# Audio tower on one core: the order of Gram products, tile 1's remainders and the first norm before the loop

## The chip, the cores and the metric

The kernel runs on one core of a Trainium2 chip. The metric is the device time of one execution in microseconds (us), and the median of several executions is what is compared. The engines are named as the profile names them: PE (matrix multiplication), PEld (its weight loads), DVE (vector), ACT (scalar), POOL (GpSimd), and SP, which issues most transfers. Each works through its own list of instructions in order, and they wait for one another on semaphores.

## The reference, cut to what matters

A path of 64 sequences by 64 steps with 8 channels is turned into signatures up to level 4, projected to 128 features, and followed by an attention block and a mixture of experts:

```python
h = _L0_tok_ref(x, L0_tok_W, L0_tok_b)          # signatures: levels 1..4, then sigs @ W.T + b
h = h + _L0_attn_ref(_layernorm(h), w_qkv, u_qkv, sigma_qkv, w_out, b_out, u_out, sigma_out, temperature)
h = h + _L0_ffn_ref(_layernorm(h), gate_w, w1, w2, w3, sw1, sw2)   # top-1 of 8 experts + a shared one

# one signature step, v = increment of the path
e = [v]; e.append(_outer(e[-1], v) / (k + 1))    # k = 1..3
acc = levels[k] + e[k] + sum(_outer(levels[i], e[k - 1 - i]))

# spectral norm of w_qkv and of w_out, one step of power iteration
v = W @ u; v = v / norm(v); u2 = W.T @ v; u2 = u2 / norm(u2)
W_used = W / (v @ W @ u2) * sigma
```

The 4,096 tokens are 32 tiles of 128. All is fp32.

## The kernel before, in words

The running sums over time are matrix products with a triangular matrix (`before`, `upto`). Level 1 and level 2 are made for many tiles at once: level 2 in four groups of eight tiles (`sum_level2(n)` on PE, `add_s2(n)` on DVE). Level 3 and the level 4 input are made tile by tile: POOL or DVE writes the outer product `e3`, ACT its high part `e3h`, POOL or DVE the remainder `e3l`, PE sums both (`sum_level3`), DVE adds `g4` (`level4`, writes `u4`), PE transposes (`features`), ACT copies the high part (`uth`, `lowt`) and DVE writes the remainders (`features_lo`, writes `utl` and `lowt`). `project(s, lo, hi)` multiplies tile s by the signature weights: ten steps n, of which 0 to 4 fill bank 1 and 5 to 9 bank 2; a step with n different from 4 and 9 is three multiplications, and steps 4 and 9 (`wlow`) are two. DVE weighs the two banks by the channels (`weigh`, writes `z`), POOL adds the eight channels in three additions (`add_channels`, the tree), and PE sums over time (`accumulate`). Then comes the first norm: DVE `first_norm`, POOL a root, DVE `first_norm_finish`, which writes `xn`; PE transposes it (`x_columns`).

A loop over 32 tiles overlaps all of this: iteration i does the attention of tile i, projects tile i+2 and starts tile i+3. Before the loop stands a hand-written prologue that fills this pipeline. It also makes the products of attention weights, and the two spectral norms from Gram matrices: `gram_qkv` is twelve products of 128x128 fp32, each two passes in the trace, all summed in bank 5, and `gram_wout` does the same for `w_out`. `norm_mm` counts the norm's matrix products as done, and `norm_step` DVE's steps of the norm.

The order on each engine is that of the code. The change touches the prologue on PE (around L1459 to L1487) and on DVE (L1076 to L1092). Three waits of the prologue matter below. `project(1, 0, ...)` waits for both remainders of tile 1 (`u4_lo`). `x_columns(0)` waits for `xn_ready`, and everything behind it on PE, `sum_level3(2)` and the second half of tile 1's projection, stands behind that wait. POOL's `level3_rest(2)` computes `g4` directly behind the root, then waits for `xn_ready` before it writes `e3l`.

Of the kernel before, what the change touches and what calls it, by code (L numbers as in the profile page):

```python
# [39 lines left out]
P = 128  # L40
# [5 lines left out]
INNER = HEADS * HEAD_DIM  # L46
# [10 lines left out]
UC = C3 // P  # L57
# [6 lines left out]
SECOND_GROUP_STEPS = 17  # L64
# [14 lines left out]
def spread(ap, axis, shape):  # L79

    return ap.unsqueeze(axis).to_broadcast(shape)
# [7 lines left out]
def build(nc, x_next, x_prev, w_low, w_high, tok_b, wqkv, u_qkv, wout_t, u_columns, b_out,  # L89
          scalars, gate_t, w13_t, w2_t, sw1_t, sw2_t, square, mask_c, steps, out):  # L90
    with ExitStack() as ctx:
# [3 lines left out]
        def sem(name):  # L95
            return ctx.enter_context(nc.semaphore(name))
# [111 lines left out]
        def taker(*hosts):  # L208
# [3 lines left out]
            def take(*shape):  # L212
# [3 lines left out]
                for part in parts:  # L216
                    flat, at = part
                    if at + size <= flat.shape[1]:
# [3 lines left out]
                        if len(shape) == 1:  # L222
# [64 lines left out]
        norm_root, norm_mm, norm_step, exp_temp = (sem("norm_root"), sem("norm_matmul"), sem("norm_step"),  # L287
                                                   sem("exp_temperature"))
# [474 lines left out]
        def _(d):  # L763
# [3 lines left out]
            def step(ins):  # L767

                nonlocal n_small
                ins.then_inc(small, 1)  # L770
                n_small += 1
                return n_small

            def after(n):
                d.wait_ge(small, n)

            def remainder(out_, x_, hi, done):

                return V.tensor_tensor(out_, x_, hi.bitcast(F32), ALU.subtract).then_inc(done, 1)  # L779

            def outer(out_, left, right):
                shape = [P, left.shape[1], CHANNELS, CHANNELS]
                return V.tensor_tensor(out_.rearrange("p t (a c) -> p t a c", c=CHANNELS), spread(left, 3, shape),
                                       spread(right, 2, shape), ALU.mult)
# [11 lines left out]
            def low_outer(ts):  # L796
                return step(outer(low[:, ts, 1 + CHANNELS:LOW], t3[:, ts, :], vh[:, ts, :]))
# [5 lines left out]
            def add_s2(n, then=None):  # L803

                s2 = B[SUM_BANKS[n]][:].rearrange("p (t c) -> p t c", c=C2)
                d.wait_ge(s2_psum, n + 1)
                made = step(V.tensor_tensor(low[:, groups[n], 1 + CHANNELS:LOW],
                                            low[:, groups[n], 1 + CHANNELS:LOW], s2, ALU.add))
                if then:
                    then(made)  # L810
                if n:
                    d.wait_ge(g3_outer, 1)
                return step(V.tensor_tensor(g3[:, groups[n], :], g3[:, groups[n], :], s2, ALU.add))
# [28 lines left out]
            made = step(V.tensor_scalar(v3, v[:], 1.0 / 3.0, None, ALU.mult))  # L842
# [3 lines left out]
            made = add_s2(0, first_level3)  # L846
# [32 lines left out]
            def weigh(s, half, first=False):  # L879

                cs = slice(half * 4, half * 4 + 4)
                d.wait_ge(y_psum, 2 * s + (half + 1))
                if half == 0 and not first:
                    d.wait_ge(tree, 3 * s - 2)
                V.tensor_tensor(z[:, cs, :], B[1 + half][:].rearrange("p (c d) -> p c d", c=4),  # L885
                                spread(v[:, bass.ds(s, 1), cs].rearrange("p o c -> p (o c)"), 2, [P, 4, DIM]),
                                ALU.mult).then_inc(z_sb, 1)

            def tile_h(t):
                return one(h[:, bass.ds(t, 1), :])  # L890

            def first_norm(t):
                d.wait_ge(h_psum, t + 1)
                V.tensor_tensor(h1[:], B[3][:, P:P + DIM], tokb[:], ALU.add).then_inc(h_read, 1)  # L894
                d.wait_ge(h_read, t + 1)
                V.bn_stats(stats[:, 0, :], h1[:]).then_inc(ln1, 1)

                d.wait_ge(ln1, 3 * t + 1)
                V.tensor_tensor(tile_h(t), B[3][:, P:P + DIM], tokbout[:], ALU.add).then_inc(h_biased, 1)
                V.bn_aggr(meanvar[:, 0, :], stats[:, 0, :]).then_inc(ln1, 1)  # L900
                d.wait_ge(ln1, 3 * t + 2)
                V.tensor_scalar(rstd[:, 0, 0:1], meanvar[:, 0, 1:2], EPS, None, ALU.add).then_inc(ln1, 1)

            def first_norm_finish(t):
                d.wait_ge(rooted[0], t + 1)
                V.tensor_scalar(xn[:], h1[:], meanvar[:, 0, 0:1], rstd[:, 0, 1:2], ALU.subtract, ALU.mult) \  # L906
                    .then_inc(xn_ready, 1)
# [5 lines left out]
            def features_lo(s):  # L913
                d.wait_ge(u4_hi, 2 * s + 2)
                remainder(utl[:].rearrange("p c t -> p (c t)"), B[0][:], uth[:].rearrange("p c t -> p (c t)"),
                          u4_lo)
                rows_ = slice(C2, P)
                remainder(lowt[rows_, 0, :], B[3][rows_, 0:P], lowt[rows_, 0, :], u4_lo)
                rows_ = slice(C2 + 2 * FEW_STEP, STACKED)
                remainder(lowt[rows_, 1, :], B[3][rows_, 3 * P:], lowt[rows_, 1, :], u4_lo)  # L920
# [136 lines left out]
            made = nstep(V.tensor_tensor(gram_u, B[5][:, 0:DIM], uq[:], ALU.mult))  # L1057
# [17 lines left out]
            d.wait_ge(consts_cast, 3)  # L1075
            weigh(0, 0, True)  # L1076
            weigh(0, 1)
            rest_made = low_outer(slice(per, TILES))
            features_lo(1)
            first_norm(0)  # L1080
            first_norm_finish(0)
            after(rest_made)
            made = add_s2(1)
            assert made == SECOND_GROUP_STEPS

            d.wait_ge(norm_mm, 2)
            V.tensor_copy(gram_out, B[5][:, 0:DIM])
            made = nstep(V.tensor_copy(wu_out[:], B[5][:, DIM:DIM + 1]))
            assert made == OUT_COLUMN_STEP
            V.tensor_tensor(nrm[:, 0:1], ucol[:, 0:1], wtwu[:], ALU.mult)  # L1090
            V.tensor_tensor(nrm[:, 1:2], wtwu[:], wtwu[:], ALU.mult)
            V.tensor_tensor(nrm[:, 2:3], wu_out[:], wu_out[:], ALU.mult)  # L1092
# [2 lines left out]
            made = nstep(V.tensor_tensor(nrm[:, 3:4], wu_out[:], B[5][:, DIM + 1:DIM + 2], ALU.mult))  # L1095
            assert made == SUMS_STEP
            made = add_s2(3)
# [7 lines left out]
            made = nstep(V.tensor_tensor(fac[:, 2:4], B[6][:, 256:260][:, 0:4:2], fac[:, 6:8], ALU.mult))  # L1105
# [110 lines left out]
        def _(pe):  # L1216
# [23 lines left out]
            def weight_products(banks, left, right):  # L1240

                for c in range(PAIRS):
                    for n in range(2):
                        rows_ = slice(n * HEAD_DIM, (n + 1) * HEAD_DIM)
                        last = mm(banks[n][:, col(c)], wqkv_sb[rows_, left + c, :], right[rows_, c, :])
                        if c == PAIRS - 1:
                            last.then_inc(ww_psum, 1)

            def gram_qkv():

                nq = 3 * INNER // P
                for c in range(nq):
                    last = mm(B[5][:, 0:DIM], wqkv_sb[:, c, :], wqkv_sb[:, c, :], c == 0, c == nq - 1)
                last.then_inc(norm_mm, 1)

            def gram_wout():

# [7 lines left out]
            def sum_level3(s):  # L1265


                pe.wait_ge(e3_lo, s + 1)
                mm(B[0][:], before_r[:], e3h[:], True, False)
                mm(B[0][:], before_r[:], e3l[:], False, True).then_inc(s3_psum, 1)  # L1270
# [12 lines left out]
            def project(s, lo, hi):  # L1283

                if lo == 0:
                    pe.wait_ge(z_sb, 2 * s)
                    pe.wait_ge(u4_hi, 2 * s + 2)
                    pe.wait_ge(u4_lo, 3 * s + 3)
                for n in range(lo, hi):
                    half_, c = divmod(n, UC + 1)  # L1290
                    bank, cols = B[1 + half_][:], col(half_, 512)
                    if c < UC:
                        mm(bank, uth[:, c, :], whigh[:, 0, c, cols], c == 0, False)
                        mm(bank, uth[:, c, :], whigh[:, 1, c, cols], False, False)
                        mm(bank, utl[:, c, :], whigh[:, 0, c, cols], False, False)
                    else:
                        mm(bank, lowt[:, 0, :], wlow[:, 0, cols], False, False)
                        mm(bank, lowt[0:STACKED, 1, :], wlow[0:STACKED, 1, cols], False, True).then_inc(y_psum, 1)
# [160 lines left out]
            sum_level2(0)  # L1459
            pe.wait_ge(ld_w, 16)  # L1460
            weight_products(B[6:8], PAIRS, wqkv_sb[:, 0:PAIRS, :])
            pe.wait_ge(before_cast, 1)
            sum_level3(0)
            pe.wait_ge(ld_sq, 32)
            features(0, False)
            gram_qkv()
            project_first_hi(0)
            sum_level3(1)
            pe.wait_ge(ld_wo, 16)
# [9 lines left out]
            pe.wait_ge(ww_lo, 2)  # L1479
            sum_level2(3)  # L1480
            gram_wout()
            project(1, 0, 1)
            accumulate(0)
            project(1, 1, UC + 1)
            pe.wait_ge(norm_step, OUT_COLUMN_STEP)
            mm(B[5][:, DIM + 1:DIM + 2], gram_out, wu_out[:]).then_inc(norm_mm, 1)
            x_columns(0)  # L1487
# [169 lines left out]
```

## Time and profile before

| | |
|---|---|
| median of 3 executions | 667.78 us (665.4 to 669.15) |
| profiled execution, its own time | 667.03 us |
| its span | 665.2 us |
| PE busy | 639.6 us, 96% of the span |
| DVE, POOL, ACT busy | 62%, 48%, 43% |
| share of PE in the chain that ended last | 91% |
| prologue, start to the first matmul of iteration 0 | 45.01 us |

Rows of the timeline give the start in us from the span's start, the length in us, the engine and line, the operation with its tiles, and in brackets the engine's idle time just before and what ended it. A length of PE counts to the modelled end of the last matmul of the row, so the difference of two starts is the better measure of work. The profile shows fp32 matmuls of 128x128 as two passes each. `PEclk` is the TensorE clock that was granted, where 1.00 stands for 2.4 GHz and 0.50 for 1.2 GHz.

### The profile page before, as it was taken

The numbers are of one execution on the slowest core, as the hardware profiler recorded it, in microseconds if no ns is written. First come the engines' busy times: TensorE is split into PE (matmuls) and PEld (weight loads), VectorE is DVE, ScalarE is ACT, GpSimd is POOL, SyncE is SP. The second block draws the span as 40 slices with busy tenths as digits, with TensorE's granted clock in tenths as the row PEclk, the third lists the DMA queues.
The fourth block names the chain that finished last, engine by engine and source line by source line (L and its number), as shares of the span: only waits on it lengthen the run. The fifth ranks groups of instructions, "written<-read, shape, count | busy, mean of one in ns | idle before, by whom it ended". The sixth has DMA issues, their size and how long they took to land.

```text
span 665.2 us, 14412 instructions
## 1 busy us (share of the span) xinstructions
PE 639.6 (96%) x4269; PEld 535.5 (81%) x4270; DVE 411.6 (62%) x1064; ACT 286.1 (43%) x655; POOL 320.6 (48%) x336
## 2 busy tenths in 40 slices
PE   5999999999999999999999999999998999999993
PEld 3777888878888878888878888877678999999993
DVE  7966666666666666666666667687646224455550
ACT  4334444454444454444444444453473433344431
POOL 2455444545444545444545444545747105555553
PEclk9989999999999999999999999999999999999997
DMA  8611433443633443433443433111337322333330
GB/s 304 237 69 30 109 80 79 113 93 83 139 79 79 114 92 83 107 79 80 114 92 83 107 79 80 41 35 45 100 97 243 94 64 38 47 46 45 44 47 2
DMA packets 70133, 59.70 MB, mean 90 GB/s; under 512 B 6752, under 2 KB 58848, under 8 KB 69728
## 3 DMA queue, kind: packets, MB, share of 16 engines
q1 hardware_dynamic: 63472, 55.21, 32.5%
q0 software_dynamic: 6640, 4.22, 4.7%
q8 instruction: 12, 0.20, 0.1%
q14 instruction: 9, 0.07, 0.0%
HBM read 16.78 MB, written 26.30 MB: 65 GB/s over the span
## 4 chain that ended last, share of the span: by engine, by line
PE 91%; DVE 4%; POOL 2%; issue 1%; ACT 0%; DMA 0%; DVEq 0%; SPq 0%; POOLq 0%
PE bank L1220 83%; PE bank L1276 2%; PE bank L1433 2%; PE bank L1403 1%; POOL z L472 1%; PE bank L1531 1%; PE bank L1326 1%; PE bank L1335 1%; PE bank L1281 1%; PE bank L1280 1%; POOL z L474 0%; DVE z L885 0%; DVE ident_b L1068 0%; DMA h<-x_prev 0%; DVE whigh L779 0%
## 5 line engine op out<-in xcount | busy, mean ns | idle before, releaser
L1220 PE MATMUL bank<-whigh,uth 128*128 128x512 f32 x512 | 169.1, 411 | 1.2 <-DVE lowt L779 1.2
L1220 PEld LDWEIGHTS bank<-whigh,uth 128*128 128x128 f32 x512 | 92.2, 190 | 28.0 <-issue 7.4
L1220 PE MATMUL bank<-whigh,utl 128*128 128x512 f32 x256 | 101.7, 397 | 0.0
L559 POOL DMA_INDIRECT out<-prob,ids x39 | 60.7, 1557 | 78.2 <-ACT prob L740 76.5
L481 POOL TENSOR_TENSOR rstd<-rstd,powers 128x1 f32<-128x1 f32 x64 | 35.2, 550 | 123.5 <-DVE rstd L872 67.3
L472 POOL TENSOR_TENSOR z<-z 128x512 f32<-128x512 f32 x32 | 42.1, 1316 | 89.6 <-DVE z L885 89.6
L1220 PE MATMUL bank<-xvo,x 128*128 128x128 f32 x624 | 76.3, 275 | 0.5 <-DVE x L1175 0.3
L1220 PEld LDWEIGHTS bank<-xvo,x 128*128 128x128 f32 x624 | 72.8, 192 | 0.9 <-DVE x L1175 0.4
L1220 PE MATMUL bank<-xT,qkw 128*128 128x128 f32 x512 | 62.5, 275 | 1.0 <-ACT pt L645 1.0
L1220 PEld LDWEIGHTS bank<-xT,qkw 128*128 128x128 f32 x512 | 59.7, 192 | 1.5 <-issue 1.4
L1191 DVE TENSOR_TENSOR z<-tail,bank 128x512 f32<-128x512 f32 x39 | 26.8, 688 | 50.6 <-PE bank L1220 50.6
L1220 PEld LDWEIGHTS bank<-whigh,utl 128*128 128x128 f32 x256 | 48.5, 189 | 12.0
L885 DVE TENSOR_TENSOR z<-bank,v 128x512 f32<-128x512 f32 x64 | 44.2, 691 | 20.4 <-PE bank L1220 16.6
L633 ACT ACTIVATE prob<-prob 128x512 f32<-128x512 f32 x32 | 20.2, 633 | 63.6 <-DVE prob L1011 63.6
L611 ACT ACTIVATE xqk<-bank,fac 128x512 f32<-128x512 f32 x64 | 44.0, 689 | 7.8 <-PE bank L1220 6.5
L645 ACT COPY pt<-bank 128x512 f32<-128x512 f32 x32 | 18.8, 586 | 65.8 <-PE bank L1433 65.8
L1220 PEld LDWEIGHTS bank<-xvp,pt 128*64 128x64 f32 x512 | 30.1, 137 | 18.1 <-issue 18.1
L467 POOL TENSOR_TENSOR e3l<-e,e3h 128x512 fp32r<-128x512 f32 x31 | 40.4, 1304 | 6.7 <-DVE xn L906 5.4
L894 DVE TENSOR_TENSOR h<-bank,tokb 128x128 f32<-128x128 f32 x32 | 9.3, 292 | 54.4 <-PE bank L1220 54.3
L1220 PE MATMUL bank<-vow,xTh 128*128 128x512 f32 x128 | 42.9, 416 | 0.0
L620 ACT COPY xvo<-bank 128x512 f32<-128x512 f32 x64 | 37.6, 588 | 10.6 <-PE bank L1220 8.9
L1220 PE MATMUL bank<-levels,z 128*128 x312 | 41.5, 276 | 0.0
(223 smaller groups left out, 1319.3 us busy)
## 6 DMA issues: line engine op xcount, KB each, us to landing
sorted_rows<-blank SPq DMA_DIRECT2D x24, 709.5 KB, 5.9
xvp<-xvo SPq DMA_DIRECT2D x128, 128.0 KB, 2.3
w<-w_t SPq DMA_DIRECT2D x1, 4096.0 KB, 12.1
xvo<-sorted_rows SPq DMA_DIRECT2D x39, 64.5 KB, 1.8
w<-w_high SPq DMA_DIRECT2D x4, 512.0 KB, 6.3
x_columns<-x2t SPq DMA_DIRECT2D x32, 64.0 KB, 1.6
xg_in<-x_columns SPq DMA_DIRECT2D x8, 256.0 KB, 4.9
levels<-w_t SPq DMA_DIRECT2D x1, 2048.0 KB, 8.9
```

What stands on the lines that cost most here:

```text
L467: G.tensor_tensor(e3l[:], e3[:], e3h[:].bitcast(F32), ALU.subtract).then_inc(e3_lo, 1)
L472: G.tensor_tensor(z4[:], z[:, 0:4, :], z[:, 4:8, :], ALU.add).then_inc(tree, 1)
L481: G.tensor_tensor(rstd[:, n, 1:2], rstd[:, n, 0:1], powers[:, 0:1], ALU.pow) \
L559: nc.gpsimd.indirect_dma_start(out=out[:, :], out_offset=bass.IndirectOffsetOnAxis(ap=ids[:, j:j + 1], axis=0), in_=y[:, 2 if j == SORTED ...
L611: A.activation(xqk[:, :, 4 * n:4 * n + 4, :], B[5 + n][:].rearrange("p (s h k) -> p s h k", s=2, h=4), ACT.Copy, scale=fac[:, 1:2]).then_i ...
L620: A.copy(xvo[:, n, :, :].rearrange("p c d -> p (c d)"), B[7 - 2 * n][:]) \
L633: A.activation(prob[:], prob[:], ACT.Exp).then_inc(exp_done, 1)
L645: A.copy(pt[:].rearrange("k c s q -> k (c s q)"), B[6][:]).then_inc(pT_sb, 1)
L885: V.tensor_tensor(z[:, cs, :], B[1 + half][:].rearrange("p (c d) -> p c d", c=4), spread(v[:, bass.ds(s, 1), cs].rearrange("p o c -> p (o ...
L1191: V.tensor_tensor(hidT[:, k, :, :].rearrange("p c t -> p (c t)"), act[:, k, :], B[2 + 2 * k][:], ALU.mult).then_inc(hid_done, 1)
L1220: return T.matmul(out_, lhsT, rhs, start=start, stop=stop)
L1276: T.transpose(B[0][:, col(c)], u4[:, col(c)], ident)
```

## The change

It moves instructions of the prologue, and adds or removes none. On PE the twelve Gram products of `wqkv` are cut in three pieces (3, 2 and 7), two of which go ahead of and behind the first level 3 sum, and `accumulate(0)` goes from behind the first step of tile 1's projection to behind the third. On DVE tile 1's remainders go ahead of the outer product of the other 24 tiles, the copies of the second Gram product go ahead of the second group's level 2 sums, and the first norm goes behind those.

```diff
+            features_lo(1)
             rest_made = low_outer(slice(per, TILES))
-            features_lo(1)
-            first_norm(0)
-            first_norm_finish(0)
-            after(rest_made)
-            made = add_s2(1)
-            assert made == SECOND_GROUP_STEPS
-
             d.wait_ge(norm_mm, 2)
             V.tensor_copy(gram_out, B[5][:, 0:DIM])
             made = nstep(V.tensor_copy(wu_out[:], B[5][:, DIM:DIM + 1]))
             assert made == OUT_COLUMN_STEP
+            after(rest_made)
+            made = add_s2(1)
+            assert made == SECOND_GROUP_STEPS
+            first_norm(0)
+            first_norm_finish(0)
...
-            def gram_qkv():
+            def gram_qkv(lo, hi):
...
-                for c in range(nq):
+                for c in range(lo, hi):
...
             weight_products(B[6:8], PAIRS, wqkv_sb[:, 0:PAIRS, :])
+            gram_qkv(0, 3)
             pe.wait_ge(before_cast, 1)
             sum_level3(0)
+            gram_qkv(3, 5)
             pe.wait_ge(ld_sq, 32)
             features(0, False)
-            gram_qkv()
+            gram_qkv(5, 3 * INNER // P)
...
-            project(1, 0, 1)
+            project(1, 0, 3)
             accumulate(0)
-            project(1, 1, UC + 1)
+            project(1, 3, UC + 1)
```

On PE, at the first level 3 sum, the list before reads as follows (`w` is the buffer of `wqkv`; the first row is the weight products, `low_tile` the last transposes of tile 0):

```order
L1220 MATMUL bank<-w 128x128 x8
L1220 MATMUL bank<-e3h,before_r 128x512
L1220 MATMUL bank<-e3l,before_r 128x512
L1276 MATMUL bank<-sq,u 128x128 x4
L1280 MATMUL bank<-sq,low_tile 128x128
L1281 MATMUL bank<-sq,low_tile 128x128
L1220 MATMUL bank<-w 128x128 x12
```

And in the changed kernel:

```order
L1219 MATMUL bank<-w 128x128 x11
L1219 MATMUL bank<-e3h,before_r 128x512
L1219 MATMUL bank<-e3l,before_r 128x512
L1219 MATMUL bank<-w 128x128 x2
L1276 MATMUL bank<-sq,u 128x128 x4
L1280 MATMUL bank<-sq,low_tile 128x128
L1281 MATMUL bank<-sq,low_tile 128x128
L1219 MATMUL bank<-w 128x128 x7
```

Three Gram products have gone ahead of the sum and two ahead of the transposes, and seven are left behind them. Lines of the changed kernel are one lower here.

On PE, at tile 1's first half, before (`z,sq` is `accumulate(0)`, `xn` is `x_columns(0)`):

```order
L1220 MATMUL bank<-whigh,uth 128x512 x2
L1220 MATMUL bank<-whigh,utl 128x512
L1220 MATMUL bank<-z,sq 128x128
L1220 MATMUL bank<-whigh,uth 128x512 x2
L1220 MATMUL bank<-whigh,utl 128x512
L1220 MATMUL bank<-whigh,uth 128x512 x2
L1220 MATMUL bank<-whigh,utl 128x512
L1220 MATMUL bank<-whigh,uth 128x512 x2
L1220 MATMUL bank<-whigh,utl 128x512
L1220 MATMUL bank<-wlow,lowt 128x512 x2
L1220 MATMUL bank<-wu_out,x2t 128x1
L1326 MATMUL bank<-sq,xn 128x128
```

And in the changed kernel:

```order
L1219 MATMUL bank<-whigh,uth 128x512 x2
L1219 MATMUL bank<-whigh,utl 128x512
L1219 MATMUL bank<-whigh,uth 128x512 x2
L1219 MATMUL bank<-whigh,utl 128x512
L1219 MATMUL bank<-whigh,uth 128x512 x2
L1219 MATMUL bank<-whigh,utl 128x512
L1219 MATMUL bank<-z,sq 128x128
L1219 MATMUL bank<-whigh,uth 128x512 x2
L1219 MATMUL bank<-whigh,utl 128x512
L1219 MATMUL bank<-wlow,lowt 128x512 x2
L1219 MATMUL bank<-wu_out,x2t 128x1
L1326 MATMUL bank<-sq,xn 128x128
```

`accumulate(0)` has moved behind six more multiplications; five instead of eleven are left between it and the product with `wu_out`.

On DVE, behind tile 0's weighing (the first common row), before and after in one piece (L783 is the outer product of 24 tiles, L779 the remainders, L807 and L813 are `add_s2(1)`):

```order
 L885 TENSOR_TENSOR z<-bank,v 128x512 x2
+L779 TENSOR_TENSOR utl<-bank,uth 128x512
+L779 TENSOR_TENSOR lowt<-bank,lowt 64x128
+L779 TENSOR_TENSOR lowt<-bank,lowt 9x128
 L783 TENSOR_TENSOR levels<-x,vh 128x24x64
-L779 TENSOR_TENSOR utl<-bank,uth 128x512
-L779 TENSOR_TENSOR lowt<-bank,lowt 64x128
-L779 TENSOR_TENSOR lowt<-bank,lowt 9x128
-L894 TENSOR_TENSOR h<-bank,tokb 128x128
-L896 BN_STATS stats<-h 128x6
-L899 TENSOR_TENSOR h<-bank,tokbout 128x128
-L900 BN_AGGR meanvar<-stats 128x2
```

The remainders come first now, and the norm (L894 on) no longer follows them; it stands behind the outer product, two copies and `add_s2(1)`.

## Rows read from the trace of the kernel before

**Rows 1.** The page: busy time of each engine.

```profile
PE 639.6 (96%) x4269; PEld 535.5 (81%) x4270; DVE 411.6 (62%) x1064; ACT 286.1 (43%) x655; POOL 320.6 (48%) x336
```

**Rows 2.** Windows inside the loop: stretch and its length, busy times, PEclk, DMA.

```profile
100.00:300.00 200.00, 200.00 (x1250) 160.35 (x1250) 131.97 (x365) 89.74 (x210) 97.60 (x112) 1.00 0.41 95
```

**Rows 3.** Timeline of PE from the weight products to tile 0's projection.

```profile
11.54 0.76 PE L1220 MATMUL bank<-e3h,before_r 128*128 128x512 f32 x1 [1.15 <-DVE e3l L849]
...
13.61 1.08 PE L1276 MATMUL bank<-sq,u 128*128 128x128 f32 x4 [0.88 <-DVE u L829]
...
14.91 4.47 PE L1220 MATMUL bank<-w 128*128 128x128 f32 x24
19.14 0.48 PE L1220 MATMUL bank<-whigh,uth 128*128 128x512 f32 x1
```

**Rows 4.** Timeline of DVE around the first Gram matrix.

```profile
17.68 0.62 DVE L779 TENSOR_TENSOR lowt<-bank,lowt 64x128 fp32r<-64x128 f32 x2
19.49 0.29 DVE L1057 TENSOR_TENSOR x2n<-bank,uq 128x128 f32<-128x128 f32 x1 [1.19 <-PE bank L1220]
```

**Rows 5.** Timeline of PE from tile 1's projection to iteration 0.

```profile
33.82 0.71 PE L1220 MATMUL bank<-whigh,uth 128*128 128x512 f32 x2 [1.24 <-DVE lowt L779]
...
34.95 0.49 PE L1220 MATMUL bank<-z,sq 128*128 128x128 f32 x2 [0.19 <-POOL z L476]
...
40.31 0.48 PE L1220 MATMUL bank<-e3h,before_r 128*128 128x512 f32 x1
...
41.56 0.62 PE L1220 MATMUL bank<-whigh,uth 128*128 128x512 f32 x2
...
42.26 0.63 PE L1220 MATMUL bank<-whigh,uth 128*128 128x512 f32 x2
...
45.01 1.95 PE L1220 MATMUL bank<-xT,qkw 128*128 128x128 f32 x16
```

**Rows 6.** Windows of one us around the fall of the clock, columns as in rows 2.

```profile
35.00:36.00 1.00, 1.00 (x4) 0.85 (x5) 0.49 (x2) 0.04 (x1) 0.93 (x1) 0.69 0.76 328
36.00:37.00 1.00, 1.00 (x4) 0.76 (x3) 0.63 (x4) 0.95 (x3) 0.22 (x1) 0.50 0.01 0
...
38.00:39.00 1.00, 1.00 (x4) 0.77 (x4) 1.00 (x2) 0.00 (x0) 0.77 (x2) 0.61 0.03 8
```

**Rows 7.** Timeline of ACT: high part of tile 1.

```profile
30.57 0.38 ACT L590 CAST lowt<-bank 128x256 fp32r<-128x256 f32 x1
```

**Rows 8.** Timeline of DVE from the outer product to the norm's columns.

```profile
30.68 1.74 DVE L783 TENSOR_TENSOR levels<-x,vh 128x1536 f32<-128x1536 f32 x1
32.35 0.68 DVE L779 TENSOR_TENSOR utl<-bank,uth 128x512 fp32r<-128x512 f32 x1
...
35.48 0.29 DVE L894 TENSOR_TENSOR h<-bank,tokb 128x128 f32<-128x128 f32 x1 [1.80 <-PE bank L1220]
...
37.38 1.10 DVE L906 TENSOR_SCALAR xn<-h,meanvar,rstd 128x128 f32<-128x128 f32 x1 [0.68 <-POOL rstd L481]
38.41 0.68 DVE L807 TENSOR_TENSOR levels<-levels,bank 128x512 f32<-128x512 f32 x1
...
39.60 0.28 DVE L1087 COPY x2t<-bank 128x128 f32<-128x128 f32 x1
...
39.98 0.16 DVE L1090 TENSOR_TENSOR nrm<-ucol,wtwu 128x1 f32<-128x1 f32 x1
```

**Rows 9.** Timeline of POOL: the tree, the root, g4 and e3l.

```profile
30.84 2.71 POOL L472 TENSOR_TENSOR z<-z 128x512 f32<-128x512 f32 x1 [3.09 <-DVE z L885]
...
34.44 0.46 POOL L476 TENSOR_TENSOR z<-z 128x128 f32<-128x128 f32 x1
...
36.78 0.57 POOL L481 TENSOR_TENSOR rstd<-rstd,powers 128x1 f32<-128x1 f32 x1 [0.85 <-DVE rstd L902]
37.34 1.07 POOL L461 TENSOR_TENSOR g<-levels,vh 128x512 f32<-128x512 f32 x1
38.63 1.28 POOL L467 TENSOR_TENSOR e3l<-e,e3h 128x512 fp32r<-128x512 f32 x1 [0.23 <-DVE xn L906]
```

More of the change, by code:

```diff
@@ L1247, in weight_products @@
                             last.then_inc(ww_psum, 1)
-            def gram_qkv():
+            def gram_qkv(lo, hi):
                 nq = 3 * INNER // P
-                for c in range(nq):
+                for c in range(lo, hi):
                     last = mm(B[5][:, 0:DIM], wqkv_sb[:, c, :], wqkv_sb[:, c, :], c == 0, c == nq - 1)
-                last.then_inc(norm_mm, 1)
+                if hi == nq:
+                    last.then_inc(norm_mm, 1)
             def gram_wout():
```

## The prediction

> **What bounds the kernel now.** I read the page first. PE is busy 96% of the span [rows 1], and in the loop it is busy without a gap at the full clock: 200.00 of 200 us [rows 2]. So whatever starts the loop earlier or later by some amount moves the end by that amount, and nothing in this change touches the loop itself. What is to be found is when iteration 0 begins; now it is 45.01 us [rows 5]. I then read the timelines of the prologue, engine by engine, for PE's gaps. There are gaps of 1.15 and 0.88 us around the first level 3 sum [rows 3], one of 1.24 before tile 1's projection and one of 0.19 before `accumulate(0)` [rows 5]. Last I read the windows: the clock goes from 1.00 to 0.69 and 0.50 about one and a half microseconds after the 1.24 gap has ended, stays at 1.2 GHz, and is back in the stretch that begins at 38 [rows 6]. By the shares of those windows it fell at 35.4 and rose at 38.8: some 3.4 us at half speed, which cost about 1.7 us of work.
>
> **Gram products.** PE did the twelve in 19.14 - 14.91 = 4.23 us, 0.176 per pass [rows 3]. Three products are six passes, 1.06 us, and fit the gap of 1.15. Two are 0.70 and fit the gap of 0.88. If those passes are slower because the clock is still low there, up to 0.22 each (as the six transposes from 13.61 to 14.91 took [rows 3]), they overrun the first gap by 0.15 us and the second not at all; the remainder e3l is what the sum waits for anyway. So tile 0's transposes stay at 13.61, and the seven left end at about 14.91 + 14 x 0.176 = 17.4 (up to 18.0). PE can't use all of this. Next comes tile 0's projection, which waits for DVE's last remainder; that ends at 17.68 + 0.62 = 18.30 [rows 4]. PE begins at 18.45 in place of 19.14: **-0.7 us on PE**, and a new gap of 0.5 to 1 us, more if the clock rises early, stands before it. DVE's wait of 1.19 us for the first Gram matrix [rows 4] goes, so DVE is 1.2 us earlier from there. That is also what the outer product on POOL and the weight remainders follow. PE has no gap from 19.14 to 32.58, the start of the 1.24 gap, so its 0.7 arrives there whole: PE is free for tile 1 at 31.9.
>
> **Tile 1's remainders.** DVE ends the weighing of tile 0 at about 30.77 now, as POOL's tree starts at 30.84 [rows 9]; 1.2 earlier is 29.6, and PE's banks allow it. ACT has the high parts of tile 1 at 30.57 + 0.38 = 30.95 [rows 7], with PE's 0.7 at 30.25. Then the remainders run at 30.3, without the outer product's 32.35 - 30.68 = 1.67 us ahead of them [rows 8]. From their start to PE's start it takes 33.82 - 32.35 = 1.47 [rows 5, 8], so 31.8; PE itself is free at 31.9. **Tile 1's projection starts at 31.9 in place of 33.82, -1.9 us, and the 1.24 gap is gone**, and with it the reason for the fall of the clock at 35.3.
>
> **accumulate(0).** Nine multiplications are ahead of it instead of three. A step of three takes 42.26 - 41.56 = 0.70 at the full clock [rows 5], so PE is there at 34.0. Is the tree ready? Now it starts at 30.84 and its first addition takes 2.71 [rows 9], ending 1.2 behind the end of the outer product at 32.35. I read this as POOL having waited for DVE's outer product. In the change the outer product starts at 31.6 at the earliest and falls among the tree's three additions. Whether they wait for each other or not, from the start at 29.7 the tree can't take longer than its 4.1 us now (30.84 to 34.90 [rows 9]) plus some tenths: 33.9 at the latest, 32.3 without a wait. Both are before 34.0. So `accumulate(0)` is at 34.05 in place of 34.95: -0.9.
>
> **The norm behind it decides.** DVE could take the sum at 34.6 (0.53 behind `accumulate(0)`, as 35.48 behind 34.95 [rows 5, 8]). But it now stands behind the outer product (31.6, pushed to about 31.75 by POOL, + 1.67 = 33.4), the two copies (39.98 - 39.60 = 0.38) and `add_s2(1)` (39.60 - 38.41 = 1.19) [rows 8]: 35.0. So the norm starts at 35.0 in place of 35.48, -0.45. From here on the chain is the same: statistics, root at +1.30 (36.78), POOL's g4 directly behind it, `xn`, then e3l, which ends at 38.63 + 1.28 = 39.91, 4.43 behind the norm's start [rows 8, 9]. That gives 39.5 for `sum_level3(2)` in place of 40.31: **-0.8**.
>
> For the `xn` step I take 1.10 [rows 8]. It lies over g4, from 37.34 to 38.41 [rows 9], and DVE's next instruction starts at 38.41. The order of both engines is unchanged here, so g4 will be ahead of it again. The Trainium skill ("SBUF — State Buffer", Who interferes with whom) says that DVE in a two-port mode and GpSimd exclude each other for a whole instruction, whoever is first. By that rule the 1.10 stays, and the trace agrees with it in this row; if the two could overlap, `xn` would come up to 0.8 us earlier and the norm's wait on PE would shrink by as much, though e3l would still stand behind g4.
>
> **What PE does meanwhile.** Behind `accumulate(0)` only five multiplications (1.2 us) and the small product with `wu_out` are left, whose column DVE has written at 33.8. PE is out of work at about 35.8 and waits in `x_columns(0)` for `xn` until 38.0, then in `sum_level3(2)` until 39.5. That is some 3.5 us of gaps with a transpose between them, where before there were 1.24 + 0.19 and 0.46 us. The twelve multiplications of tile 1's second half stand behind these waits. The stall has moved, not gone.
>
> From `sum_level3(2)` to iteration 0 it is 45.01 - 40.31 = 4.70 us at the full clock [rows 5]. After a gap of 1.24 the clock was at half speed for 3.4 us; after 3.5 us of gaps I expect it to fall as well, at some point around 38 to 39, and to stay down for about as long. The part that falls on work, 2.5 to 3.4 us at half speed, costs 1.3 to 1.7; I take 1.5. Iteration 0 then starts at 39.5 + 4.7 + 1.5 = 45.7 in place of 45.01. **The sum is +0.7 us** (-0.8 for the chain, +1.5 for the clock).
>
> The Trainium skill ("TensorE: Matmul & The Clock Gate", What's actually happening) has the same rule: idle time halves the clock, and only sustained activity restores it. It speaks against this change, since it turns two short gaps into one long one.
>
> **Its size.** The profiled execution took 667.03 by its own time, so 667.7; against the median of 667.78 it is 668.5. The two anchors differ by as much as the sum, so I put down 668.2. A difference of 0.5%, 3.3 us, is about what a measurement of this kernel can tell from no change; the three runs of before spread over 3.7 us.
>
> **Rivals.**
> 1. *The gain arrives whole (chance 0.15).* The clock doesn't fall, or not while PE has work, as PE has been busy without a gap from 18.45 to 35.8. Then only the chain counts: -0.8, 666.2 to 667.0. If in addition `xn` came earlier (the norm's 4.43 us has 1.07 of g4 in it), it would be up to -1.9, 665.1 to 665.9. For it speaks that the 1.24 gap vanishes; against it the chain through the norm, in which no row gets shorter.
> 2. *The clock stays low through all of tile 1's second half (0.25), the slower side.* It decides if the clock doesn't return until `features(2)`. Fourteen multiplications of 512 columns and the transposes, the 4.7 us, then cost up to 4.7 more: -0.8 + 4.7 = +3.9 at the worst, 670.9 to 671.7; with return half way +2, 669.0 to 669.8. For it speaks that PE is idle for most of 35.8 to 39.5; against it that the low stretch of before ended while PE worked on.
> 3. *The change does nothing that shows (0.1).* The new gap before 18.45 makes the clock fall there as well, by the same 1.7 us that the old gap cost later, or the DVE's outer product is pushed behind the tree, so that the norm starts at 35.5. Then all moves cancel: 667.0 to 668.0.
> 4. *The forecast (0.5):* the norm starts 0.45 earlier, the clock falls behind the new wait and comes back: +0.2 to +1.5, 667.2 to 669.3.
>
> **How the numbers follow.** None of the four cases is sure to leave the band of 3.3 us; only the worst end of rival 2 (+3.9) does, and the scatter of runs adds to it. Faster by over 0.5% has 0.05, the tail of rival 1 with the scatter. Slower by over 0.5% has 0.09. The rest is 0.86 for within 0.5%. The range leaves out the ends of rivals 1 and 2: 665.9 to 670.6.
>
> **What would show it.** Right: tile 1's projection starts near 31.9 without a gap; DVE goes from L779 (`lowt`, 18.3) to L1057 at once; `x_columns(0)` has a gap of about 2 us released by `xn`, and PEclk is at 0.5 somewhere between 38 and 43; iteration 0 starts between 45 and 46.5. Wrong: a start of `first_norm` before 34.7 (then DVE wasn't the limit), no fall of the clock (rival 1), or half clock up to iteration 0 (rival 2). A change in the loop's own period would be outside all of this.

## The result and the profile after

The change is slower by 0.3%: ratio of the changed kernel to the kernel before 1.0032, 95% interval [1.0019, 1.0046], medians 668.70 us and 667.62 us over ten executions each. Those medians are 1.1 us apart and the means 1.7, where the ratio stands for 2.1 us, so the size is less sure than the sign. Run again in a later series it gave 1.0036 [1.0021, 1.0050]. The forecast was 668.2 us, 0.5 below the median, and the range of 665.9 to 670.6 held it.

The profiled execution of the changed kernel has a span of 665.5 us. Its timeline of PE, with the rows that answer to [rows 3] and [rows 5]:

```profile
11.49 0.47 PE L1219 MATMUL bank<-e3h,before_r 128*128 128x512 f32 x1 [0.54 <-DVE e3l L849]
...
13.30 0.63 PE L1276 MATMUL bank<-sq,u 128*128 128x128 f32 x4 [0.65 <-DVE u L829]
...
13.98 1.73 PE L1219 MATMUL bank<-w 128*128 128x128 f32 x14
17.99 0.47 PE L1219 MATMUL bank<-whigh,uth 128*128 128x512 f32 x1 [2.29 <-issue]
...
31.34 0.70 PE L1219 MATMUL bank<-whigh,uth 128*128 128x512 f32 x2
...
33.52 0.38 PE L1219 MATMUL bank<-z,sq 128*128 128x128 f32 x2
...
37.66 0.47 PE L1326 MATMUL bank<-sq,xn 128*128 128x128 f32 x1 [2.47 <-DVE xn L906]
39.07 0.80 PE L1219 MATMUL bank<-e3h,before_r 128*128 128x512 f32 x1 [0.94 <-POOL e3l L467]
...
45.92 1.95 PE L1219 MATMUL bank<-xT,qkw 128*128 128x128 f32 x16
```

The seven Gram products left (14 passes) end early, and PE then has a gap of 2.29 us before tile 0's projection, for which the profile names no releaser; DVE's last remainder of tile 0 ends at 17.9. The 1.24 gap before tile 1's projection is gone: it starts at 31.34 in place of 33.82, and `accumulate(0)` at 33.52 in place of 34.95. Then come the two new waits, 2.47 us for `xn` and 0.94 for `e3l`. Of the lead of 2.48 us at 31.34, 1.24 is left at `sum_level3(2)` (39.07 against 40.31), and at iteration 0 PE is 0.91 us late (45.92 against 45.01). The windows say what became of it, with the columns of rows 2:

```profile
36.00:37.00 1.00, 0.00 (x0) 0.00 (x0) 0.49 (x1) 0.00 (x0) 1.00 (x2) 0.99 0.00 0
37.00:38.00 1.00, 0.34 (x1) 0.18 (x1) 1.00 (x5) 0.00 (x0) 0.77 (x2) 0.50 0.00 0
42.00:43.00 1.00, 1.00 (x4) 0.80 (x3) 0.00 (x0) 0.00 (x0) 0.00 (x0) 0.50 0.00 0
43.00:44.00 1.00, 1.00 (x4) 0.77 (x3) 0.00 (x0) 0.00 (x0) 0.00 (x0) 0.59 0.00 0
```

The clock fell to 1.2 GHz at 37.0, in the middle of the wait for `xn`, and rose again at 43.8. `sum_level3(2)` to iteration 0 took 6.85 us in place of 4.70, 2.15 more. The span is only 0.3 us longer than before (665.5 against 665.2), though iteration 0 is 0.91 us late: the loop's 31 steps to the last iteration take the same 438.3 us, and what stands behind them took 0.7 us less here. So one profile shows the prologue well and the total badly.

DVE and POOL answer to [rows 4], [rows 8] and [rows 9]:

```profile
17.92 0.29 DVE L1057 TENSOR_TENSOR x2n<-bank,uq 128x128 f32<-128x128 f32 x1
...
29.85 0.69 DVE L779 TENSOR_TENSOR utl<-bank,uth 128x512 fp32r<-128x512 f32 x1 [0.65 <-ACT lowt L590]
...
31.23 1.76 DVE L783 TENSOR_TENSOR levels<-x,vh 128x1536 f32<-128x1536 f32 x1
...
34.61 0.28 DVE L894 TENSOR_TENSOR h<-bank,tokb 128x128 f32<-128x128 f32 x1
...
36.51 1.09 DVE L906 TENSOR_SCALAR xn<-h,meanvar,rstd 128x128 f32<-128x128 f32 x1 [0.68 <-POOL rstd L481]
```

```profile
29.28 1.27 POOL L472 TENSOR_TENSOR z<-z 128x512 f32<-128x512 f32 x1 [3.09 <-DVE z L885]
...
31.43 1.88 POOL L476 TENSOR_TENSOR z<-z 128x128 f32<-128x128 f32 x1
...
37.74 1.27 POOL L467 TENSOR_TENSOR e3l<-e,e3h 128x512 fp32r<-128x512 f32 x1 [0.23 <-DVE xn L906]
```

L1057 follows without a wait, and the norm (L894) starts without one too: DVE comes to it only at 34.61, though `accumulate(0)` was at 33.52. The tree's first addition takes 1.27 us now in place of 2.71, and its third 1.88 in place of 0.46, since it lies over the outer product, which starts at 31.23. So the collision has moved from the first addition to the third.

### The profile page after: what moved, and what is told of

Same layout as the page of the kernel before. It is cut to its first block, busy times and chain, and to the rows that moved or that the text cites. A ratio compares the mean times of both kernels' runs of the same rounds, so it can differ in the third digit from the quotient of the medians.

```text
span 665.5 us, 14380 instructions
## 1 busy us (share of the span) xinstructions
PE 632.4 (95%) x4237; PEld 533.9 (80%) x4270; DVE 411.5 (62%) x1064; ACT 286.1 (43%) x655; POOL 320.9 (48%) x336
## 4 chain that ended last, share of the span: by engine, by line
PE 91%; DVE 3%; issue 2%; POOL 1%; ACT 1%; DMA 0%; SPq 0%; POOLq 0%; DVEq 0%
PE bank L1219 84%; PE bank L1276 2%; PE bank L1433 2%; PE bank L1533 1%; PE bank L1335 1%; PE bank L1326 1%; PE bank L1281 1%; PE bank L1280 1%; DVE levels L783 0%; POOL z L472 0%; DMA h<-x_prev 0%; POOL z L474 0%; POOL out L559 0%; DVE z L885 0%; DVE levels L807 0%
## 5 line engine op out<-in xcount | busy, mean ns | idle before, releaser
L894 DVE TENSOR_TENSOR h<-bank,tokb 128x128 f32<-128x128 f32 x32 | 9.3, 291 | 52.6 <-PE bank L1219 52.5
```

## The experiments

Theory A: PE's waits for `xn` and `e3l` stand in front of tile 1's second half, nothing shortens the chain that ends them, and the clock falls behind them. The rivals were that the Gram cut itself costs (C), that something behind the wait is as late (B), and that the half clock costs nothing. The ratio given is to the kernel before, run beside it on the same chip.

**The Gram cut alone.** The kernel before with this:

```diff
             weight_products(B[6:8], PAIRS, wqkv_sb[:, 0:PAIRS, :])
+            gram_qkv(0, 3)
             sum_level3(0)
+            gram_qkv(3, 5)
             features(0, False)
-            gram_qkv()
+            gram_qkv(5, 3 * INNER // P)
```

> The kernel before with only the cut of the Gram products (3, 2 and 7). Theory A (the cost lies in PE's wait for xn and e3l in front of tile 1's second half, and in the half clock behind it): this part is a gain by itself. DVE loses its wait of 1.19 us for the first Gram matrix, tile 1's projection starts 0.7 to 1.2 us earlier than 33.82, iteration 0 at 43.8 to 44.3 in place of 45.01, ratio to before 0.998 to 0.999. Rival C (the new gap of about 2.3 us before tile 0's projection costs, by the clock or by what it delays): iteration 0 not earlier than 45.0, ratio 1.000 or above.

Measured: 0.9980 [0.9971, 0.9989]. In the timeline of PE iteration 0 starts at 43.63, 1.38 us earlier than before, though the same gap of 2.3 us stands before tile 0's projection:

```profile
17.99 0.47 PE L1220 MATMUL bank<-whigh,uth 128*128 128x512 f32 x1 [2.30 <-issue]
...
32.26 0.71 PE L1220 MATMUL bank<-whigh,uth 128*128 128x512 f32 x2 [0.83 <-DVE lowt L779]
...
38.62 0.38 PE L1220 MATMUL bank<-wu_out,x2t 128*128 128x1 f32 x2 [0.62 <-DVE wu_out L1088]
...
38.93 0.48 PE L1220 MATMUL bank<-e3h,before_r 128*128 128x512 f32 x1
...
43.63 1.95 PE L1220 MATMUL bank<-xT,qkw 128*128 128x128 f32 x16
```

This part is a gain. Its `sum_level3(2)` comes at 38.93, earlier than the whole change's 39.07, so the lead that the changed kernel has at that point is all the Gram cut's. DVE says why:

```profile
34.11 0.29 DVE L894 TENSOR_TENSOR h<-bank,tokb 128x128 f32<-128x128 f32 x1 [2.00 <-PE bank L1220]
```

The norm starts at 34.11 here, and at 34.61 where the other moves are added: they bring `accumulate(0)` no gain that the norm could use (33.38 here, 33.52 there) and put `add_s2(1)` ahead of the norm.

**The rest without the Gram cut.** The changed kernel with `gram_qkv()` in one piece again.

> The changed kernel with the Gram products back in one piece of twelve. Theory A: everything is about 1 us later than in the changed kernel and the wait for xn stays, so iteration 0 at 46.5 to 47.2, ratio to before 1.003 to 1.006. Rival C: without the gap before tile 0's projection it is better than the changed kernel, iteration 0 before 45.9, ratio to before 1.002 or below.

Measured: 1.0042 [1.0029, 1.0055]. Timeline of PE:

```profile
39.60 0.47 PE L1325 MATMUL bank<-sq,xn 128*128 128x128 f32 x1 [2.52 <-DVE xn L906]
41.02 0.80 PE L1219 MATMUL bank<-e3h,before_r 128*128 128x512 f32 x1 [0.94 <-POOL e3l L467]
...
48.18 1.95 PE L1219 MATMUL bank<-xT,qkw 128*128 128x128 f32 x16
```

The loss is all in the rest. The ratio is the expected one, and in the profile iteration 0 is later than expected (48.18, where at most 47.2 was): `sum_level3(2)` at 41.02 is even behind the 40.31 of before, and from there it is 7.16 us to iteration 0. Of the delay 0.39 us is there at tile 0's projection (19.53 in place of 19.14). C falls, by the ratio too; that the Gram cut may have a cost of its own in some executions comes below.

**The second half first.** The changed kernel with tile 1's steps 5 to 8 ahead of the waits:

```diff
+            project(1, UC + 1, 9)
             x_columns(0)
             sum_level3(2)
-            project(1, UC + 1, 9)
```

> The changed kernel with steps 5 to 8 of tile 1's projection ahead of x_columns(0) and sum_level3(2). Theory A: the 12 multiplications (2.8 us) fill the wait of 2.47 us; sum_level3(2) stays near 39.0, behind it only the norm's product, the last two multiplications and the transposes are left, which wait for DVE's u4 until about 41.1; iteration 0 at 41.8 to 42.5 (43.5 if the clock still falls), ratio to before 0.993 to 0.997. Rival B (the wait for xn isn't what limits, since something behind it, such as DVE's level 2 sums, the norm's steps or the tree of tile 1, ends as late): iteration 0 or the accumulate behind it moves by less than 1.5 us against the changed kernel, ratio to before 0.999 to 1.002.

Measured: 0.9982 [0.9970, 0.9994], 0.5% better than the change, and between the figures of theory A (up to 0.997) and of B (from 0.999). The wait for `xn` is gone; `x_columns(0)` starts without one. Iteration 0 came at 44.62, not at 42.5, because this profile has two falls of the clock. Windows in each of them, and PE's first row of iteration 0:

```profile
20.00:22.00 2.00, 2.00 (x6) 1.17 (x4) 2.00 (x3) 0.00 (x0) 0.00 (x0) 0.50 0.00 0
44.00:46.00 2.00, 2.00 (x11) 2.00 (x10) 1.76 (x7) 0.86 (x2) 0.48 (x1) 0.50 0.00 0
```

```profile
44.62 2.96 PE L1219 MATMUL bank<-xT,qkw 128*128 128x128 f32 x16
```

The first (19.4 to 22.8) follows a gap of 2.39 us before tile 0's projection, the one that the Gram cut makes. Against the first profile of the change iteration 0 moved by 1.30 us, which B would allow. Against the change's profile that has the early fall as well (48.16, further down) it is 3.54 us earlier. B falls by that: what stands behind the wait could start earlier.

**A filler in the waits.** The changed kernel with

```diff
+            for _ in range(10):
+                mm(B[0][:], uth[:, 0, :], whigh[:, 0, 0, 0:512])
             x_columns(0)
+            for _ in range(3):
+                mm(B[0][:], uth[:, 0, :], whigh[:, 0, 0, 0:512])
             sum_level3(2)
```

> The changed kernel with 10 extra multiplications of 512 columns ahead of x_columns(0) and 3 ahead of sum_level3(2), all into a bank that is free there and is overwritten; they do no work of the reference and only keep PE busy while it would wait. Theory A with the clock: sum_level3(2) stays at 39.1, PEclk stays at 1.00 through 37 to 44, and iteration 0 comes at 43.8 in place of 45.92; ratio to before 0.997 to 0.999, that is 2 us better than the changed kernel. Rival (the half clock isn't caused by the wait, or costs nothing): the clock falls all the same or iteration 0 stays at 45.9, ratio to before 1.002 to 1.005.

Measured: 1.0029 [1.0014, 1.0044], no better than the change, and the rival's figure. The profile had 1.00 from 24 to 50, but its first product started at 5.04 in place of 3.8 us and the clock fell at 19.8 for 3.4 us. The same kernel was profiled again:

> The same kernel as the filler in the wait for xn and e3l, once more, for its profile: its first product started 1.2 us later than in all other profiles, behind the transfer of the triangular matrix. If that was chance, the product is at 3.8 us now and iteration 0 is at 43.8 to 45.5; if it belongs to this program, the product is at 5.0 again, and that explains why its median isn't better than the changed kernel's.

One execution, 666.38 us. It has the first product at 3.91 and the full clock throughout, and iteration 0 where theory A put it; its windows from tile 0's projection on, and PE:

```profile
25.00:44.00 19.00, 18.58 (x96) 14.57 (x95) 15.67 (x34) 2.29 (x7) 9.78 (x9) 1.00 0.45 195
```

```profile
39.17 0.50 PE L1219 MATMUL bank<-e3h,before_r 128*128 128x512 f32 x1 [0.41 <-POOL e3l L467]
43.88 1.95 PE L1219 MATMUL bank<-xT,qkw 128*128 128x128 f32 x16
```

`sum_level3(2)` is where it was (39.17 against 39.07) and iteration 0 2.04 us earlier. So the wait belongs to the chain and the 2 us behind it to the clock. The late start was no property of the program.

Why is the ratio no better, then? The last iteration's first product, in the changed kernel and in this one:

```profile
484.25 2.02 PE L1219 MATMUL bank<-xT,qkw 128*128 128x128 f32 x16 [0.97 <-ACT pt L645]
```

```profile
483.81 2.02 PE L1219 MATMUL bank<-xT,qkw 128*128 128x128 f32 x16 [0.96 <-ACT pt L645]
```

From iteration 0 to here it is 438.33 us in the changed kernel and 439.93 with the filler: of the 2.04 us gained 1.6 are lost in the loop, whose instructions are the same. All three profiles of this program show it (439.9 to 440.0), and none of the other eleven does (438.2 to 438.7), the one with both fillers included (438.25). Why this program's loop is slower isn't shown; the rival was right about the total, and not about the clock.

**The norm ahead of the level 2 sums.** The changed kernel with `first_norm(0)` and `first_norm_finish(0)` ahead of `add_s2(1)`.

> The changed kernel with the first norm ahead of the second group's level 2 sums again (the copies of the Gram product stay ahead of both). Theory A: the norm no longer waits for DVE, it starts when accumulate(0) is read, 0.5 to 0.6 us earlier (34.0 to 34.1 if the first clock doesn't fall), and the gap before x_columns(0) shrinks to about 1.9 us; sum_level3(2) at 38.5; the clock still falls. Ratio to before 1.002, 0.6 us better than the changed kernel. Rival (the place of the norm on DVE is the main cost): the gap goes and the ratio is 1.000 or below.

Measured: 1.0017 [1.0000, 1.0034]. Its first product came at 5.23, 1.40 us later than the 3.83 of the change. DVE now waits 0.66 us for PE before the norm, and on PE:

```profile
38.50 0.37 PE L1326 MATMUL bank<-sq,xn 128*128 128x128 f32 x1 [1.90 <-DVE xn L906]
39.91 0.80 PE L1219 MATMUL bank<-e3h,before_r 128*128 128x512 f32 x1 [1.04 <-POOL e3l L467]
```

39.91 less the late start is 38.51, as expected, and the ratio is near the expected 1.002. The norm's place on DVE is worth 0.56 us of the chain; the gap shrinks from 2.47 to 1.90 and doesn't go.

**Fillers in the early gap as well.** The previous filler, and between the Gram products and tile 0's projection:

```diff
             gram_qkv(5, 3 * INNER // P)
+            for c in range(10):
+                mm(B[1][:, 0:DIM], wqkv_sb[:, c, :], wqkv_sb[:, c, :])
             project_first_hi(0)
```

> The changed kernel with filler multiplications in the wait for xn and e3l (as in the run before) and ten more Gram products, into a bank that is free, in the gap of 2.3 us before tile 0's projection; neither does work of the reference. Theory A with the clock: PEclk stays at 1.00 from the first Gram products to iteration 0 in the profile; against the filler in the later wait alone, where the clock fell at 19.9 to 23.1, the run is 1 to 1.7 us better: ratio to before 0.999 to 1.001. Rival (fillers cost as much as they save, as the first filler run suggests, since its median is no better than the changed kernel's): ratio 1.002 to 1.005.

Measured: 1.0010 [0.9998, 1.0022]. Its profile has the full clock to iteration 0, which starts at 44.66 after a first product at 4.69. Against the change's own 1.0032, of another series, that is 0.2% better, at the upper end of what was expected. The profile's span was still 668.5 us. At the end of the loop, where PE waits in every one of the kernels, the clock fell here and not in the kernel before. The windows of this kernel:

```profile
480.00:485.00 5.00, 3.54 (x17) 3.03 (x18) 1.93 (x9) 3.86 (x8) 2.62 (x3) 0.80 0.31 96
485.00:490.00 5.00, 4.34 (x27) 3.52 (x28) 0.20 (x2) 3.86 (x9) 3.83 (x4) 0.85 0.26 67
```

Six of the fourteen profiles have such a fall between 483 and 509 us, and from the last iteration's start to the end they take 182.6 to 185.6 us, the other eight 180.4 to 181.9. This one is the 185.6; the fall accounts for at most 1.8 us of that, and the rest isn't explained. The six are six programs, with and without fillers, so what brings that fall on isn't shown either.

**The second half first, with the early filler.** Both edits above (without the fillers in the waits).

> The changed kernel with tile 1's second half ahead of x_columns(0), and ten filler Gram products in the gap before tile 0's projection. Theory A with the clock: no fall of the clock at 19 to 23, iteration 0 at 42 to 43, ratio to before 0.993 to 0.997, 1 to 2 us better than the second half alone (0.998). Rival (the early gap's clock fall doesn't reach the end, since DVE and POOL set the pace there): ratio 0.998 as without the filler.

Measured: 0.9960 [0.9948, 0.9973], the expected 0.2% better than without the filler, though of another series and with intervals that just overlap. The clock stays up to 41.2, and iteration 0 starts at 42.23, as theory A had it.

**The change and its filler on one chip.** The changed kernel again:

> The changed kernel itself once more, on the same chip as the three others of this call, to set the fillers against it. Both theories: ratio to before 1.002 to 1.004. Its profile shows whether the clock falls in the gap before tile 0's projection, which it didn't in the first profile; if it does, the wait for xn comes 1 us later.

Measured: 1.0036 [1.0021, 1.0050]. This profile is the less lucky one. Windows and PE:

```profile
19.00:20.00 1.00, 1.00 (x4) 0.78 (x3) 1.00 (x1) 0.59 (x1) 0.00 (x0) 0.59 0.09 33
22.00:23.00 1.00, 1.00 (x11) 0.72 (x12) 1.00 (x2) 0.00 (x0) 0.00 (x0) 0.71 0.00 0
```

```profile
18.41 0.47 PE L1219 MATMUL bank<-whigh,uth 128*128 128x512 f32 x1 [2.38 <-issue]
...
40.96 0.79 PE L1219 MATMUL bank<-e3h,before_r 128*128 128x512 f32 x1 [0.99 <-POOL e3l L467]
...
48.16 1.95 PE L1219 MATMUL bank<-xT,qkw 128*128 128x128 f32 x16
```

The clock fell behind the early gap too, and iteration 0 is at 48.16, 2.24 us later than in the first profile of the same program. Its eight executions lie in two groups: three at 667.4 to 668.1 us with a mean clock of 0.990, five at 670.0 to 670.3 with 0.984 to 0.987. The first group is 0.8 us above the mean of the kernel before (666.85), the second 3.3.

The two profiles of this program differ before the gap already. The first level 3 sum:

```profile
11.75 0.75 PE L1219 MATMUL bank<-e3h,before_r 128*128 128x512 f32 x1
12.32 0.42 PE L1219 MATMUL bank<-e3l,before_r 128*128 128x512 f32 x1
```

From one start to the next it is 0.57 us here and was 0.31 (11.49 to 11.80) in the first profile: here PE came up to its full pace only during the sum, there it had done so ahead of it. `PEclk` reads 1.00 for that stretch in both, so only the rows show it.

 The filler in the waits, beside it:

> The filler in the wait for xn and e3l, against the changed kernel on one chip. Theory A with the clock: 1 to 2 us better than the changed kernel (ratio to before 1.000 to 1.001). Rival (what is saved at the clock is lost elsewhere in most executions): no better than the changed kernel, ratio 1.002 to 1.004, as in its first runs.

Measured: 1.0023 [1.0010, 1.0036], mean 668.36 us against 669.19 for the change. The direction is as expected, but 0.83 us is less than the 1 to 2 expected, the ratio is in the rival's range, and the intervals overlap. Its profile has the early fall, and then the 4.73 us from 40.93 to 45.66 at the full clock, where the change took 7.20; its loop is the 1.7 us slower one. So the clock's 2 us in the prologue are shown by the profiles, and the totals neither prove nor refute them.

**All gaps filled.** The second half first, the early filler, three multiplications ahead of `sum_level3(2)` and two ahead of `features(2)`.

> The changed kernel with tile 1's second half ahead of x_columns(0), fillers in the gap before tile 0's projection (ten Gram products), ahead of sum_level3(2) (three multiplications) and ahead of the last transposes (two); the fillers do no work of the reference. Theory A with the clock: no fall of the clock before the loop's end, iteration 0 at 42.2 as before but no half clock in it, ratio to before 0.992 to 0.995, about 1 us better than with the first filler alone (0.996). Rival (the falls are paid only now and then): 0.996 again.

Measured: 0.9958 [0.9947, 0.9970]. No fall of the clock up to 45, iteration 0 at 41.72:

```profile
39.05 0.50 PE L1219 MATMUL bank<-e3h,before_r 128*128 128x512 f32 x1 [0.19 <-POOL e3l L467]
...
41.72 1.98 PE L1219 MATMUL bank<-xT,qkw 128*128 128x128 f32 x16
```

It is the best kernel here, but the ratio is the rival's figure: the last two fillers can't be told from nothing (0.9960 without them).

**The old gap filled.** The kernel before, with a filler in its 1.24 gap:

```diff
+            pe.wait_ge(z_sb, 2)
+            pe.wait_ge(u4_hi, 4)
+            for _ in range(5):
+                mm(B[1][:], uth[:, 0, :], whigh[:, 0, 0, 0:512])
             project(1, 0, 1)
             accumulate(0)
```

> The kernel before with five filler multiplications in its gap of 1.24 us ahead of tile 1's projection, nothing else. Theory A with the clock: the projection starts at 33.8 as before, the clock stays at 1.00 from 35 to 39, iteration 0 at 43.3 in place of 45.0, ratio 0.998 to 0.999 as the clock fell there only in a part of the executions. Rival (the fall isn't caused by the gap): the clock falls all the same, ratio 1.000.

Measured: 1.0007 [0.9997, 1.0016], a miss for theory A as I had put it. The clock did stay up from 35 to 39, and then this happened on PE:

```profile
34.67 0.49 PE L1220 MATMUL bank<-z,sq 128*128 128x128 f32 x2 [0.20 <-POOL z L476]
...
39.70 0.38 PE L1220 MATMUL bank<-wu_out,x2t 128*128 128x1 f32 x2 [1.97 <-DVE wu_out L1088]
40.01 0.48 PE L1220 MATMUL bank<-e3h,before_r 128*128 128x512 f32 x1
...
46.24 1.95 PE L1220 MATMUL bank<-xT,qkw 128*128 128x128 f32 x16
```

With the full clock PE was done with tile 1's first half earlier and waited 1.97 us, where in the kernel before it waited 0.46. From `accumulate(0)` to `sum_level3(2)` it is 40.01 - 34.67 = 5.34 us, and it was 40.31 - 34.95 = 5.36 at half clock [rows 5]. The half clock of the kernel before had cost nothing. The executions fit, though a mean clock doesn't say where it fell: in each of the three later series those of the kernel before with a mean clock of 0.989 or less took 666.3 to 666.4 us on the mean, and those with 0.994 or more 667.1 to 667.6. Behind the new wait of 1.97 us the clock then fell, from 41.0 to 44.4, on work that does count.

## Why the prediction was right, and where not

**The chain through the norm was the right step.** In every kernel with the whole change or its second part, `sum_level3(2)` waited for it; in the kernel before and with the Gram cut alone the same chain reached PE through DVE's column for the norm (L1088), a few tenths ahead. The norm started at 34.61 (35.0 in the working) and `e3l` was read 4.46 us behind it (4.43 + latency). "The stall has moved, not gone" is what the rows show: 2.47 and 0.94 us, 3.41 together, where 3.5 were named.

**Gram products.** The step said -0.7 us on PE and a gap of 0.5 to 1 us, more if the clock rises early. It did rise early: 14 passes took 1.7 us in place of the 2.5 assumed, and the gap was 2.29. The 0.176 per pass was a mean of two paces, 0.21 up to about 18.5 us and 0.11 behind that; in the first profile of the changed kernel PE had the fast pace from the first level 3 sum on. The six transposes, which the working left at 13.61 and at 0.22 each, started at 13.30 and took 0.68 us in all. The projection began at 17.99, 1.15 us earlier and not 0.7, because DVE was ready for the last remainder 0.4 us earlier too (it now ends at 17.9 in place of 18.3), behind the shorter sum and transposes. By itself the part gave 1.38 us at iteration 0 and a ratio of 0.9980.

**Tile 1's start** at 31.34 (31.9), **accumulate(0)** at 33.52 (34.05): both half a microsecond better, for the reason just given. The tree was indeed ready in time. The Trainium skill ("SBUF — State Buffer", Who interferes with whom) says that a DVE instruction with two SBUF inputs contends with a GpSimd instruction that reads SBUF, and that in a two-port mode whoever issues first has the shared ports for its whole instruction. The trace agrees in three rows: the `xn` step took 1.09 over `g4` as the 1.10 of before, the tree's first addition got 1.4 us shorter once the outer product no longer ran beside it, and its third 1.4 us longer.

**What the -0.8 was put down to.** The size held, and more (1.24 us at `sum_level3(2)`). But the working added up the whole change and didn't ask what the Gram cut gives alone: with that the norm starts at 34.11, 1.4 us earlier than before, and the other moves put it back to 34.61. They are where the loss comes from.

**The clock behind the new wait: right in kind, too small.** The working had 1.5 us; it cost 2.15 (6.85 against 4.70). The stretch took 4.7 us in all three profiles with the filler in the waits and 6.9 to 7.2 in the four that had the waits unfilled in the old order.

**What was wrong: the price of the old fall.** The prediction said that the 3.4 us at half speed before "cost about 1.7 us of work". It cost nothing at iteration 0, since PE had slack of that size in front of the norm's column; filling the gap turned it into a wait of 1.97 us. The sum of +0.7 hadn't counted a gain from it, but rival 3 set it off against the fall in the early gap, and there was nothing to set off.

**What the sum left out.** It was made from one profile with one fall of the clock. The early gap of 2.3 us, made by the Gram cut, lets the clock fall in some executions: in four of the eight profiles that had the cut and no early filler. Where it did, iteration 0 came 2.2 us later in the changed kernel. One in two makes about 1 us on the mean, and 0.9 + 1 is near the 2.1 us of the ratio 1.0032. Rival 3 named this fall as a way to no change; it was a part of the forecast case instead. The executions fit: those of the changed kernel with a mean clock of 0.989 or 0.990 are 0.8 us above the mean of the kernel before in both series, which is the sum of +0.7, and those with 0.984 to 0.987 are 2.7 and 3.3 above. So the number 668.2 is met partly by luck, as the mean of a good case and a worse one that the sum didn't hold.

How often it falls is an estimate from few profiles. What goes with it is the start: in the four profiles with the early fall the two products of the first level 3 sum start 0.40 to 0.57 us apart, in the four without it 0.30 to 0.31. In the three with the early filler they are 0.31 apart too, so their full clock doesn't show that the filler prevents the fall; for that there are only the ratios (0.9960 against 0.9982). Which of the two, a late rise or the gap, decides isn't settled here.

The size of each part, on the ratio: the Gram cut -0.2%, the rest +0.4%. The sum is less than the +0.3% measured for both, by about what the intervals allow.

## What to carry to other kernels

When a wait disappears, walk the same engine's list forward to the next wait whose end nothing has moved: an engine that arrives earlier only waits longer there, unless work that doesn't depend on it is put in front. Here that was one line, the second half of tile 1 ahead of `x_columns(0)`, and it turned +0.3% into -0.2% (-0.4% with the early gap filled). A stretch at half clock costs only what the engine's slack behind it doesn't cover, so price it at the next wait, not by its length; and a gap can cost twice where the work behind it is on the critical path. A single profile holds one draw of these falls; look at the mean clock of all executions before the parts are summed, and before a filler is judged by its total, compare the length of the loop that it shouldn't touch.

## What the runs showed of the hardware

The first matrix product started between 3.8 and 5.2 us in the fourteen profiles, in four of them 0.8 us late or more, behind the transfer of the triangular matrix; that alone can move one execution by up to 1.4 us.

The same program with the same gaps shows a fall of the clock in one execution and none in the next: the changed kernel behind its gap of 2.3 us at 16 us. "TensorE: Matmul & The Clock Gate" of the Trainium skill (What's actually happening) says that recent busyness sets the clock and that low activity halves it; the falls in the prologue all followed gaps, which agrees, and the same gap did not always have one.

The same loop of 31 steps took 438.3 us in the changed kernel and 439.9 to 440.0 in the three profiles of the program with thirteen more products ahead of it.
